# A two-layer graph network on one core: numbering of rows and columns so that the 128 rows of a transfer are adjacent

## What is computed

```python
def lap_mul(A, x):
    d = 1.0 / sqrt(sum(A, axis=-1))
    return d[:, None] * (A @ (d[:, None] * x))

h = maximum(layernorm(x), 0)
z = leaky_relu(lap_mul(adj, h) @ W1 + b1, 0.1)
S = exp(-sqrt(pairwise_sq_distance(z) + 1e-10) / 2)
S = S where it is among the 4 largest of its row, else 0
x = x + (lap_mul(S + adj, h) @ W2 + b2)
h = maximum(layernorm(x), 0)
x = x + (h @ W[:, :128].T + (adj @ h) @ W[:, 128:].T + b)
```

## Time and profile before

| | us |
|---|---|
| median of 3 runs | 1177.01 |
| lowest, highest | 1172.3, 1194.65 |
| the profiled execution, its own time | 1180.82 |
| its span, first to last instruction | 1178.8 |

### The profile page before, as it was taken

One profiled execution on the slowest core, in us unless ns is written; L12 is line 12 of the kernel. 1 busy time (PEld: TensorE's weight loads), 2 busy tenths in 40 slices (PEclk: granted clock), 3 DMA queues, 4 the chain that ended last, 5 costly groups with the idle time before them and its releaser, 6 DMA issues.

```text
span 1178.8 us, 12596 instructions
## 1 busy us (share of the span) xinstructions
PE 929.5 (79%) x3378; PEld 583.5 (50%) x3378; DVE 868.9 (74%) x960; ACT 566.7 (48%) x1171; POOL 680.8 (58%) x1103
## 2 busy tenths in 40 slices
PE   0146437549559788769999999979989997999997
PEld 0023213224224333346766766435656645788886
DVE  2648558757768999747999998627687648888884
ACT  2454434545422221147777778424334433676763
POOL 9999988878673668104555565667777763000000
PEclk9987679689789888979999999999999998899999
DMA  9999999999999999739766767998989997699992
GB/s 210 293 315 321 330 331 363 341 335 359 361 333 358 339 313 356 296 125 367 260 250 247 256 235 270 395 412 316 349 299 356 371 341 269 248 369 383 376 387 90
DMA packets 98750, 369.10 MB, mean 313 GB/s; under 512 B 21264, under 2 KB 34320, under 8 KB 73872
## 3 DMA queue, kind: packets, MB, share of 16 engines
q1 hardware_dynamic: 51696, 258.43, 56.6%
q0 software_dynamic: 40960, 103.87, 30.7%
q10 hardware_dynamic: 6048, 6.29, 1.6%
HBM read 244.78 MB, written 123.73 MB: 313 GB/s over the span
## 4 chain that ended last, share of the span: by engine, by line
PE 41%; DVE 7%; POOL 5%; issue 4%; DMA 3%; ACT 2%; POOLq 0%; ACTq 0%; DVEq 0%
PE ps L1362 6%; PE ps L1380 5%; PE ps L1381 5%; PE ps L1382 5%; PE ps L1363 5%; PE ps L1364 5%; PE ps L1389 4%; POOL zt_lo L613 3%; PE ps L1359 2%; DVE araw_r L1207 2%; DVE araw L936 1%; DMA araw<-in_adj_dram 1%; DVE out_t L1164 1%; PE ps L1259 1%; PE ps L1271 1%
## 5 line engine op out<-in xcount | busy, mean ns | idle before, releaser
L389 POOL DMA_DIRECT2D araw<-in_adj_dram x704 | 382.7, 552 | 88.5 <-DVE tr L936 48.9
L1207 DVE TENSOR_TENSOR araw_r<-araw,tr_r 128x512 fp32r<-128x512 f32 (+1 forms) x184 | 213.9, 1220 | 63.4 <-ACT tr_r L815 63.3
L815 ACT ACTIVATE tr_r<-araw 128x2048 fp32r<-128x2048 f32 x88 | 166.3, 1910 | 74.4 <-DMA araw<-transposed 29.6
L613 POOL DMA_INDIRECT zt_lo<-neighbour_table,idx_st x128 | 144.2, 1126 | 48.8 <-issue 42.3
L761 ACT ACTIVATE araw<-ps,nsq 128x1024 f32<-128x1024 f32 x128 | 142.6, 1117 | 55.4 <-PE ps L1364 55.4
L1271 PE MATMUL ps<-tr,ys 128*128 128x512 f32 x256 | 130.7, 661 | 35.5 <-DVE ys L943 28.5
L659 ACT ACTIVATE ps<-araw 128x256 f32<-128x256 f32 x304 | 111.6, 367 | 81.9 <-DMA araw<-in_adj_dram 81.4
L936 DVE STREAM_TRANSPOSE tr<-araw 128x2048 f32<-128x2048 f32 x32 | 123.3, 3873 | 30.3 <-DMA araw<-in_adj_dram 26.7
L1389 PE MATMUL ps<-araw,ys 128*128 128x512 f32 x320 | 142.9, 602 | 2.6 <-ACT ys L806 2.6
L1362 PE MATMUL ps<-zt_lo,zs_hi 128*128 128x512 f32 x256 | 108.8, 425 | 0.0
L1066 DVE TENSOR_REDUCE bmax<-araw 128x64 f32<-128x4096 f32 x23 | 101.5, 4411 | 9.4 <-ACT araw L761 7.4
(11 more groups left out here) (164 smaller groups left out, 1460.7 us busy)
## 6 DMA issues: line engine op xcount, KB each, us to landing
araw<-transposed SPq DMA_DIRECT2D x128, 1024.0 KB, 7.1
araw<-in_adj_dram POOLq DMA_DIRECT2D x704, 128.0 KB, 16.2
keys_scratch<-araw SPq DMA_DIRECT2D x96, 512.0 KB, 3.5
transposed<-tr SPq DMA_DIRECT2D x32, 1024.0 KB, 8.6
transposed<-unit_zt_hi SPq DMA_DIRECT2D x8, 1024.0 KB, 9.3
transposed<-unit_zt_lo SPq DMA_DIRECT2D x8, 1024.0 KB, 8.7
transposed<-unit_sq_rows SPq DMA_DIRECT2D x8, 1024.0 KB, 9.5
transposed<-araw SPq DMA_DIRECT2D x8, 1024.0 KB, 5.3
```

Source lines behind the costliest of these rows:

```text
L389: gp.dma_start(araw[R * q:R * q + R, place, U * v:U * v + U], adj_v[q, :, g // 2, g % 2, v, :, c]).then_inc(a_first_in[place], DMA)
L613: gp.indirect_dma_start(out=gath[:, i, u, k, :], out_offset=None, in_=table, in_offset=bass.IndirectOffsetOnAxis(ap=idx_st[:, i, u * TOPK ...
L815: act.activation(ring_hi[:, place % TSLOTS], ring[:, j], ACT.Copy).then_inc(hi_done, 1)
L1207: ins = v.tensor_tensor(ring_lo[:, j, u], ring[:, j, u], ring_hi[:, place % TSLOTS, u].bitcast(F32), ALU.subtract)
```

## The change

The two groups of a range of 1024 rows now lie 128 rows apart within each block of 256 rows (h ahead of s), a partition has 4 adjacent rows of a group, and the tiles of a partition are adjacent rows. Columns are renumbered alike.

```diff
-    x_v = x.rearrange("(a q s u h) f -> q a h s u f", a=CHUNKS, q=QD, u=U, h=2)
-    out_v = out.rearrange("(a q s u h) f -> q h s a u f", a=CHUNKS, q=QD, u=U, h=2)
-
-    adj_v = adj.rearrange("(a v r u h) (c q k) -> q r a h v u c k", a=CHUNKS, v=QD, u=U, h=2, c=CHUNKS, q=QD)
+    x_v = x.rearrange("(a q h s u) f -> q a h s u f", a=CHUNKS, q=QD, u=U, h=2)
+    out_v = out.rearrange("(a q h s u) f -> q h s a u f", a=CHUNKS, q=QD, u=U, h=2)
+
+    adj_v = adj.rearrange("(a v h r u) (c q k) -> q r a h v u c k", a=CHUNKS, v=QD, u=U, h=2, c=CHUNKS, q=QD)
...
-                src = raw.rearrange("p m (s t h) -> p h t m s", h=CHUNK_UNITS, s=R)[:, j % CHUNK_UNITS]
+                src = raw.rearrange("p m (h s t) -> p h t m s", h=CHUNK_UNITS, s=R)[:, j % CHUNK_UNITS]
```

## The result

| | before | changed |
|---|---|---|
| median of 21 runs | 1177.8 us | 1182.83 us |
| lowest, highest | 1160.03, 1194.65 | 1167.69, 1192.02 |
| ratio, 95% interval | | 1.008, 1.0041 to 1.0118 |
| span of the profiled execution | 1178.8 | 1181.0 |

The account below looks back on a forecast made before the run. DMA bounds stage A to 350 us, DVE with DMA close behind stage B to 500 us, then PE. The span of 1178.8 minus 4 (c) and 0.5 (d) is 1176.3, less 3.8 to a median: 1172 us, range 1145 to 1201.

Parts of the forecast that it names:

- the likeliest case: Whole kernel: time stays the same within 2% (23.5 us), chance 0.66.
- (c): Load of x at the start, 2 KB instead of 512 B pieces: saves 4 us (range 1.9 to 5.1), shifting everything after.
- 130 ns a piece: Load of x: price of a 2 KB piece by the adj packet, making 8.3 us in all.
- the stores' price: Load of x: 2 KB piece at the stores' 407 GB/s, 80 ns each, making 5.1 us in all.
- (a): adj loads (L389), rows now closer in memory: zero change taken, ends 24 us less or 24 us more.
- Rivals 1 and 3: adj loads 10% faster with closer rows, 1145 us, chance 0.22; or 10% slower, 1202 us, chance 0.13 together with Rival 4.
- queue 0 alone over 275 or under 240 GB/s: Sign that the forecast is wrong: adj load rate with no other queue running; expected near 254 to 270 GB/s.
- (b): POOL's issue of adj loads: stays 552 ns each; upper end 1126 ns.
- Rival 4: POOL's adj issue takes over 0.62 us a load; at 0.70, 1218 us; chance held inside the slower adj loads' 0.13.
- (d): Stores of the output by ACT, 2 KB instead of 512 B pieces: between 0 and 1 us saved, 0.5 taken.
- (e): Transpose at L936, stride 16 B instead of 32 B: stays 3873 ns; low end about 2210 ns.
- Rival 2: Transpose gets cheap at 16 B, 2.2 us, shortening stage B: 1162 us, 10 less than forecast; chance 0.07.

Follow-up runs that it names:

- the pair of load kernels: Transfers only, no network computed: ten segments of adj loads taking every second row against a twin taking adjacent rows; means 1241.9 and 1232.3 us.
- x and output alone: Kernel before with only the new views of x and output (2 KB pieces), adj numbering old; ratio 0.9905 to before, 0.9931 when repeated.
- experiment 5: Against the kernel before, whole network renumbered so the transpose reads adjacent elements, x in 512 B pieces; ratio 0.9942, repeated 1.0069; mean 1176.0 us.

## Why the prediction was wrong, step by step

The forecast was 1172 us, 5 less than before; the outcome is a loss of 0.1 to 5.4 us by all runs. It stayed within 2%, as the likeliest case had it, but went the other way.

- **(c), the step that failed: "this time passes to the end of stage A and shifts all after it".** It failed in its path, and the term itself was too large.

  *The size.* "I take 4" was too much. SP's queue while it carries x, in the kernel before from 0 to 40 us and in the changed one from 0 to 23 us:

```profile
q1 hardware_dynamic: 4568, 2.09, 25.9%
...
q1 hardware_dynamic: 1503, 2.07, 38.9%
```

These are 10.4 and 9.0 us of all 16 engines for the same 2.1 MB; over four profiles of each kernel 10.3 and 8.7. So the larger pieces save 1.6 us. The 130 ns a piece worked out from the adj packet were right, and the stores' price, towards which the choice leaned, was not. The sum also counted the small packets of the kernel before among its 4608 and left them out of the 1024 after, which makes the saving look larger than it was.

*The path.* By 50 us the changed kernel had moved 13.2 MB (12.86, 13.27, 13.36, 13.36 in four profiles) and the kernel before 11.6 (11.60, 11.28, 11.88, 11.80). But of these 1.6 MB, 1.4 were on SP's queue (4.52 against 3.1 MB): x, the weights and the first two units. SP then has to wait for the next units, which are made of adj, and by 140 us its lead had shrunk to 0.1 MB. The loads of adj were 0.4 MB ahead by then (29.9 against 29.5), some 1.5 us at the 285 GB/s of this stretch, about what x had saved. From 140 to 345 us the loads of adj cost 2% more than before, as shown above, and by 345 us the changed kernel was 0.5 MB behind. So of the 4 us forecast at most 2.4 stood at the seventh reduction, and none at the end of the first pass. The share of 1.03 was read as "bound by DMA throughout", and a microsecond of transfer saved was booked to the end with the price of all later transfers held fixed. That price did not hold; what moved it stays open.

- **(a)** "I take zero" was right within 2 us (the pair of load kernels). Rivals 1 and 3 have no hold there, between 128 and 64 KB per partition. The row pitches of the Trainium skill ("DMA: Bandwidth & Descriptors", section Latency and other measured facts) begin at 512 KiB, and no run here tests them. The sign "queue 0 alone over 275 or under 240 GB/s" was a poor one: from 40 to 50 us, with nothing else beside it, queue 0 had 266, 272, 291 and 289 GB/s in the four changed profiles, and 241 and 281 with x and output alone, where the loads have the old rows.
- **(b)** right: 552 ns. **Rival 4** fell with it.
- **(d)** "Between 0 and 1 us": from the last addition to the end it was 1178.8 - 1173.6 = 5.2 us and is 1181.0 - 1176.8 = 4.2. The term measured 1.0 and not 0.5, at the end of its range; 0.7 of it is ACT's issue, four times 620 against 441 ns.
- **(e)** right: 3850 ns. The Trainium skill's rule of 16-byte lines ("SBUF — State Buffer", section Door 1: The DMA port swizzle) is borne out by this case as far as it goes (nothing between 4 and 16 B was run): 32 B 3873, 16 B 3850, adjacent 2296 ns for 2048 elements. The low end, put at 2210 ns, was off by 4%.
- **Rival 2** was refused for a stride of 16 B, rightly, and its price holds at a stride of 4 B: 64 x 1.58 = 101 us less of DVE, of which the whole kernel keeps 7 to 10; it had said 10. The stretch from the thirteenth reduction to L1043 fell from 171 to 160 and 164 us.
- **Noise.** The text said that 2% is what a measurement can tell; it did not ask how far the ratio of one kernel with itself lies from 1.

## What to carry to other kernels

A share of DMA engines at 1 says that they are busy, not that a byte less at the start is time less at the end: ask which queue gets the time that comes free, and follow a saving to two or three fixed marks down the trace before booking it. When a transpose or another pass over SBUF reads with a stride, look for a numbering that lets it read adjacent elements; here a transpose took the same at 16 B as at 32 B and 40% less at 4 B. And run a kernel against itself before believing a difference under 1%.

## What was not expected of the hardware

- SP's issue of a 64 KB load took 598 ns with pieces of 512 B and 421 with pieces of 2 KB; ACT's stores went from 620 to 441.
- Loads that stand behind small pieces in SP's queue wait long beside POOL's queue: with 2 KB pieces of x the weights came at 29.9 to 31.7 us (six profiles of whole kernels), with 512 B pieces at 48.3 to 50.5 us (six profiles) and, in the numbering of experiment 5, which has 512 B pieces too, at 41.8 and 42.9. So the size of the pieces is not all of it.
- The same loads in the same order spread by 6% within one execution, 119.3 to 126.4 us for a segment of 12 chunks; in the kernel whose ten segments all take every second row, a segment took 111.1 to 126.6 us.
